# Unscaled probabilities, an output scaled behind the value product, and keys projected directly, in a fused attention and gated-FFN layer

## The reference

```
xn = layernorm(x)
q = (xn @ Wq + bq) in 8 heads of 128, + pe      # pe: sinusoidal positions
k, v = halves of (xn @ Wkv + bkv); k = k + pe   # one key/value head for all query heads
probs = softmax(causal(q @ k.T / sqrt(128)))
attn = (probs @ v) @ Wo
xr, xk = mu * xn + (1 - mu) * (xn shifted by one token)
ffn = sigmoid(xr @ Wr.T) * (relu(xk @ Wk.T) ** 2 @ Wv.T)
out = x + attn + ffn
```

## Time and profile before

| | |
|---|---|
| median of 3 runs | 1531.99 us (1531.63 to 1533.14) |
| the profiled execution | 1534.33 us |
| its span, first to last instruction | 1531.7 us |
| granted TensorE clock, mean | 0.997 |
| PE busy | 1500.0 us (98%) |
| DVE busy | 1241.5 us (81%) |
| POOL busy | 1146.9 us (75%) |
| ACT busy | 1056.0 us (69%) |

### The profile page before, as it was taken

One profiled execution on the slowest core, in us unless ns is written; L12 is line 12 of the kernel. 1 busy time (PEld: TensorE's weight loads), 2 busy tenths in 40 slices (PEclk: granted clock), 3 DMA queues, 4 the chain that ended last, 5 costly groups with the idle time before them and its releaser, 6 DMA issues.

```text
span 1531.7 us, 36132 instructions
## 1 busy us (share of the span) xinstructions
PE 1500.0 (98%) x11724; PEld 1463.2 (96%) x11724; DVE 1241.5 (81%) x3393; ACT 1056.0 (69%) x2531; POOL 1146.9 (75%) x1666
## 2 busy tenths in 40 slices
PE   6999999999999999999999999999999999999998
PEld 6999999999999999999999999999999999999998
DVE  6888868888688886888868888788877887778875
ACT  5776667766677766777577666677767766766764
POOL 5787877878677777777777777778777787767864
PEclk9999999999999999999999999999999999999999
DMA  4144422444224441234413444134441344413443
GB/s 144 39 125 125 129 94 57 129 129 138 84 61 116 138 147 63 79 114 143 130 59 94 116 140 131 45 107 118 136 140 35 101 129 134 135 33 94 125 151 104
DMA packets 227001, 165.04 MB, mean 108 GB/s; under 512 B 51712, under 2 KB 222080, under 8 KB 226816
## 3 DMA queue, kind: packets, MB, share of 16 engines
q1 hardware_dynamic: 225552, 162.08, 35.3%
q10 hardware_dynamic: 1264, 0.66, 0.2%
HBM read 81.93 MB, written 77.59 MB: 104 GB/s over the span
## 4 chain that ended last, share of the span: by engine, by line
PE 77%; DVE 7%; POOL 6%; DMA 4%; issue 3%; SPq 1%; ACT 1%; ACTq 0%; DVEq 0%; POOLq 0%
PE pS L1051 25%; PE pO L1188 21%; PE pG L1051 13%; PE pG L1138 9%; PE pT L1154 7%; DMA park_dram<-Y 3%; POOL X L581 2%; POOL qt L533 2%; SPq L461 1%; DMA Z<-park_dram 1%; DVE X L1030 1%; DVE Y L939 1%; POOL pt L548 1%; DVE mix L875 1%; DVE pt L955 1%
## 5 line engine op out<-in xcount | busy, mean ns | idle before, releaser
L1051 PE MATMUL pS<-kt,qt 128*128 128x288 f32 (+41 forms) x2304 | 460.9, 330 | 3.6 <-POOL qt L533 1.9
L782 ACT ACTIVATE X<-X,bias 128x16 f32<-128x16 f32 (+56 forms) x512 | 376.3, 735 | 112.0 <-DVE bias L1030 110.5
L1188 PE MATMUL pO<-pt,v 128*128 128x256 f32 x3288 | 441.0, 284 | 1.6 <-DVE ot L1009 1.5
L1188 PEld LDWEIGHTS pO<-pt,v 128*128 128x128 f32 x3288 | 405.8, 189 | 2.5 <-DVE ot L1009 2.3
L1030 DVE CUSTOM_DVE_ANT_0 X<-pS,mask 128x16 f32<-128x16 f32 (+56 forms) x512 | 354.0, 691 | 52.6 <-PE pS L1051 45.8
L581 POOL TENSOR_SCALAR X<-X,rec 128x16 f32<-128x16 f32 (+56 forms) x512 | 371.0, 725 | 32.7 <-DVE rec L929 22.0
L548 POOL TENSOR_TENSOR pt<-Z,pt 128x256 fp32r<-128x256 f32 (+5 forms) x192 | 318.9, 1661 | 93.4 <-ACT pt L704 89.3
L1051 PEld LDWEIGHTS pS<-kt,qt 128*128 128x128 f32 x2304 | 367.4, 189 | 16.9 <-DVE bias L1030 2.4
L775 ACT CAST ot<-pO 128x256 fp32r<-128x256 f32 x256 | 96.4, 376 | 235.7 <-PE pO L1188 119.9
L955 DVE TENSOR_TENSOR pt<-pT,pt 128x512 fp32r<-128x512 f32 (+3 forms) x440 | 207.7, 493 | 32.1 <-ACT pt L711 30.6
L533 POOL TENSOR_TENSOR qt<-qtmp,qt 128x256 fp32r<-128x256 f32 x252 | 191.3, 762 | 25.0 <-ACT qt L677 18.0
(11 more groups left out here) (120 smaller groups left out, 1931.7 us busy)
## 6 DMA issues: line engine op xcount, KB each, us to landing
park_dram<-Y SPq DMA_DIRECT2D x32, 512.0 KB, 2.6
Z<-park_dram SPq DMA_DIRECT2D x128, 128.0 KB, 2.8
park_dram<-Y SPq DMA_DIRECT2D x32, 448.0 KB, 3.0
Z<-park_dram SPq DMA_DIRECT2D x128, 112.0 KB, 2.5
park_dram<-Y SPq DMA_DIRECT2D x32, 384.0 KB, 2.9
Z<-park_dram SPq DMA_DIRECT2D x128, 96.0 KB, 2.4
park_dram<-Y SPq DMA_DIRECT2D x32, 320.0 KB, 2.7
Z<-park_dram SPq DMA_DIRECT2D x128, 80.0 KB, 2.1
```

The lines of the kernel that those rows point to most:

```text
L782: nc.scalar.activation(x_row(s, 0, w), x_row(s, 0, w), ACT.Exp, bias=bias[:, j:j + 1], scale=-1.0, accum_out=total[:, j:j + 1]).then_inc(e ...
L1051: last = nc.tensor.matmul(out, a[i], m[j], start=start and k == 0, stop=stop and k == n - 1)
L1188: last = nc.tensor.matmul(pO[:, 0:2 * P], v[i][:, k, :], pt[j][:, pair % 2, k, :], start=n == 0, stop=n == 3 * nk - 1)
```

## The change

- The probabilities are no longer scaled. POOL's scaling is gone; what is left of it in an iteration is clearing the unwritten part of a row tile, and the copies of the packed diagonal part (a copy where it was a scaling). DVE takes one reciprocal for a pair (two columns) in place of two.
- The reciprocals of a pair (128 by 2) are written to DRAM by one DMA and read back to all partitions by another (`inverse`, 128 by 256). Both stand in SP's queue, at `s+3` and `s+7` of the pair's even step.
- Behind the value product DVE multiplies `pO` by `inverse` into SBUF (`o_scaled`); ACT makes the high part from it one iteration later (`O_LAG`), POOL the low part. The next value product waits for DVE's multiplication.
- Keys are projected transposed (`wkv` stationary, tokens moving) and get bias and position there; what PE transposes is now the values, which DVE copies out. Two small key tables and their additions at the start are gone; `omu` is computed on POOL.
- The lags and tables are new (`T_LAG` 6 to 5, `V_LAG` 3 to 2), and the order in an iteration: PE does WO, transposition, fillers, scores, value product; DVE does the mask before the output's multiplication; POOL does `pt` low at its end. `Z` is a ring of four units, of which a narrow step takes one.
- ACT's copy of a PE-transposed step waits for the value product of the pair two before it.

```diff
-T_LAG = 6
+T_LAG = 5
 PV_LAG = 8
-V_LAG = 3
-H_LAG = (7, 8)
+V_LAG = 2
+H_LAG = (7, 7)
+SUMS = 2
+SUMS_AT = 3
+O_LAG = 1
...
-      "mixk_dve": (6, 11, 8, 10),
-      "mixk_out": (12, 14, 10, 11)}
+      "mixk_dve": (6, 9, 7, 10),
+      "mixk_out": (13, 13, 10, 13)}
...
+            def sums_out_of(b, s):
+                k = pair_no(b, s)
+                sp.wait_ge(rec_ready, k + 1)
+                if k >= 4:
+                    sp.wait_ge(sums_landed[(k - 4) % SUMS], 16 * ((k - 4) // SUMS + 1))
+                sp.dma_start(sums_d[k % 4, :, :], rec[:, k % 4, :]
+                             ).then_inc(sums_out[k % 2], 16)
+            def sums_in(b, s):
+                k = pair_no(b, s)
+                sp.wait_ge(sums_out[k % 2], 16 * (k // 2 + 1))
+                if k >= SUMS:
+                    sp.wait_ge(o_lo, k - SUMS + 1)
+                sp.dma_start(inverse[:, k % SUMS, :, :], sums_d[k % 4:k % 4 + 1, :, :].broadcast_to((P, P, 2))
+                             ).then_inc(sums_landed[k % SUMS], 16)
             for b, it in turns():
+                if it % 2 == SUMS_AT % 2 and 0 <= it - SUMS_AT - 4 < STEPS:
+                    sums_in(b, it - SUMS_AT - 4)
+                if it % 2 == SUMS_AT % 2 and 0 <= it - SUMS_AT < STEPS:
+                    sums_out_of(b, it - SUMS_AT)
...
-                    if not scaled_by_act(s):
-                        nc.gpsimd.tensor_scalar(x_row(s, 0, w), x_row(s, 0, w), rec[:, j:j + 1], 1.0,
-                                                ALU.mult, ALU.mult).then_inc(normed, 1)
...
+                first = it - PV_LAG - 1 - O_LAG
+                if 0 <= first < STEPS and first % 2 == 0:
+                    k = pair_no(b, first)
+                    pool.wait_ge(o_hi, k + 1)
+                    nc.gpsimd.tensor_tensor(o_out[1], scaled_o(k).rearrange("p t (h q) -> p t h q", h=H),
+                                            o_out[0].bitcast(F), ALU.subtract).then_inc(o_lo, 1)
...
                 s = it - T_LAG
                 if 0 <= s < STEPS:
+                    if t_banks(s) and pair_no(b, s) > 1:
+                        act.wait_ge(pv_done, pair_no(b, s) - 1)
...
+                first = it - PV_LAG - 1
+                if 0 <= first < STEPS and first % 2 == 0:
+                    k = pair_no(b, first)
+                    dve.wait_ge(pv_done, k + 1)
+                    dve.wait_ge(sums_landed[k % SUMS], 16 * (k // SUMS + 1))
+                    nc.vector.tensor_tensor(scaled_o(k), pO[:, 0:2 * P].rearrange("p (t n) -> p t n", t=2), scaled_o(k),
+                                            ALU.mult).then_inc(o_scaled, 1)
...
-                                pe.wait_ge(o_lo, b * (STEPS // 2) + pair)
+                                pe.wait_ge(o_scaled, b * (STEPS // 2) + pair)
```

More of the change, by code:

```diff
@@ L183, in t_banks, with z_units @@
     return [] if turned(s) else [(k, min(4, n - k)) for k in range(0, n, 4)]
+def z_units():
+    unit, before, used = [], [], [None] * UNITS
+    for n in range(2 * len(TURNED)):
+        s = TURNED[n % len(TURNED)]
+        size = 1 if s < SHARED else 2
+        ends = n and unit[n - 1] + (1 if TURNED[(n - 1) % len(TURNED)] < SHARED else 2)
+        u = 0 if n % len(TURNED) == 0 else -(-ends // size) * size % UNITS
+        users = [x for x in used[u:u + size] if x is not None]
+        unit.append(u)
+        before.append(n - max(users) if users else 0)
+        used[u:u + size] = [n] * size
+    return unit[0:len(TURNED)], before
 def users_before():
@@ L209 @@
 T_BODY = T_FIRST[STEPS]
-N_FIRST = [sum((SUB * 2 if packed(r) else P) > (r % H + 1) * SUB for r in range(s))
-           + sum((not scaled_by_act(r)) + packed(r) for r in range(s)) for s in range(STEPS + 1)]
+N_FIRST = [sum(((SUB * 2 if packed(r) else P) > (r % H + 1) * SUB) + packed(r) for r in range(s))
+           for s in range(STEPS + 1)]
 N_BODY = N_FIRST[STEPS]
@@ new lines, in turn @@
+                if 0 <= s < STEPS and s % 2:
+                    k = pair_no(b, s)
+                    dve.wait_ge(exp_done, b * STEPS + s + 1)
+                    if k >= 4:
+                        dve.wait_ge(sums_out[k % 2], 16 * ((k - 4) // 2 + 1))
+                    nc.vector.reciprocal(rec[:, k % 4, :], total[:, k % 4, :]).then_inc(rec_ready, 1)
+                s = it - T_LAG
+                for w in [w for w in WITHIN if w + H_LAG[w % 2] + 1 == it]:
+                    last = w // H
+                    dve.wait_ge(turned_hi, turned_no(b, w) + 1)
+                    within = pt_of(0, w)[32:64, last, :].rearrange("p (a c) -> p a c", a=4)
+                    nc.vector.tensor_tensor(within, z_of(w, last + 1)[32:64, :, last, :], within.bitcast(F),
+                                            ALU.subtract).then_inc(within_lo, 1)
@@ new lines, in turn @@
+                if 0 <= s < STEPS:
+                    for m, (k, nk) in enumerate(t_banks(s)):
+                        u = T_FIRST[s] + m
+                        dve.wait_ge(t_hi, b * T_BODY + u + 1)
+                        full = nk - (packed(s) and k + nk == s // H + 1)
+                        if full:
+                            low = nc.vector.tensor_tensor(pt_of(1, s)[:, k:k + full, :],
+                                                          pT[u % 2][:, 0:full * P].rearrange("p (k n) -> p k n", n=P),
+                                                          pt_of(0, s)[:, k:k + full, :].bitcast(F), ALU.subtract)
+                        if full < nk:
+                            within = pt_of(0, s)[32:64, s // H, :]
+                            low = nc.vector.tensor_tensor(within, pT[u % 2][32:64, full * P:nk * P], within.bitcast(F),
+                                                          ALU.subtract)
+                        low.then_inc(t_lo, 1)
```

436 lines of the change are left out of this document (199 added, 237 removed).

## The result

| | before | changed |
|---|---|---|
| median | 1531.81 us (1530.04 to 1533.14) | 1776.12 us (1765.07 to 1780.68, 4 runs) |
| ratio, 95% interval | | 1.159 (1.157 to 1.161), slower |
| span of the profiled execution | 1531.7 us | 1763.3 us |
| PE idle in it | 31.7 us | 176.8 us |
| granted clock, mean | 0.997 | 0.967 |

A forecast was written before the change was run, and what follows sets the result against it. PE was taken as the bound, at work 1500.0 of 1531.7 us. Terms -8.7 - 1.5 - 2.4 - 2.0 + 0.45 + 1.2 = -13.0 took the profiled 1534.3 to 1521.3, the median to 1519.0 us; range 1509 to 1538.

The forecast's parts named there:

- The two DMAs of a pair: SP's queue: 512 added DMAs, the read issued some 6 us before DVE needs it; hidden, 0.
- Rival C: Spread sums come late, so DVE sits before `pO` and PE's value product behind it: 17 us, 1536; chance 0.08.
- The sign of B: In PE's list, waits of scores for DVE's `bias` or mask of more than 5 us.
- POOL: POOL's busy time falls from 1146.9 to about 971 us; FK's wait for its mix split goes, -8.7 us.
- rival A: The stall changes its owner: DVE or ACT late where POOL was, about 1530 us; chance 0.17.
- The order: PE's WO first in its iteration, fewer waits for its bank: -2.4 us; all terms together -13.0.
- rival B: Narrow steps wait for their mask behind value product, ACT's copy and DVE: 25.6 us lost, 1544.6; chance 0.11.
- dense time fixed: PE's 1500.0 us of work stay, with products as many and as wide; at most 31.7 us idle can go.
- DVE: Fewer reciprocals, a new copy of transposed values: net -27 us, busy 1205 to 1225 us, 0 on the path.
- The start: `omu` and key table leave DVE's path; POOL's mix split at 20.48 and FK come earlier: -2.0 us.
- The end: WO of the last row tile comes later, as DVE's multiplication goes first: +0.45 us.
- The clock: With PE's 1.9 us pause before the FK at 1402, the slow stretch behind it goes: -1.5 us.

The follow-up runs named there:

- e2: Changed kernel with only the write of the reciprocals, read back left out, output multiplied by a constant tile: 1744.8 us.
- e1: Changed kernel without its two small DMAs per pair, output multiplied by a constant tile instead of the reciprocals: 1553.5 us.
- e3: Changed kernel with only the read back, of a constant 1 KB row broadcast to all partitions, nothing written: 1553.7 us.
- f10: Changed kernel with the write alone, in packets of 64 bytes side by side, constant factor: 1553.8 us.
- f11: Changed kernel with the write alone, 8-byte packets each 512 bytes from the next in DRAM, constant factor: 1553.1 us.
- f9: Kernel before with POOL's split of the token mix of chunk 2 one iteration earlier: 1539.8 us.
- e7: Changed kernel without its small DMAs, constant factor, PE's value product put back ahead of the scores: 1578.8 us.
- f12: Changed kernel without its small DMAs, constant factor, WO put back behind transposition and other fillers: 1585.5 us.
- e8: Kernel before with an added write per pair, 128 packets of 8 bytes side by side to DRAM, read by nobody: 1802.1 us.
- e4: Changed kernel with both small DMAs issued from ScalarE's (ACT's) queue instead of SP's: 1853.5 us.

## Why the prediction was wrong

**The step that failed** is "The two DMAs of a pair": "None so small and so often is in the trace; the nearest land in 1.9 us (32 KB), a large one in 3.0 us ... hidden, 0." The step asked only when the new DMAs land and who waits for them. It never asked what they do to the transfers already there. The runs put this in its place: the write costs 191 us (`e2` less `e1`), with a parking that lands at 5.8 in place of 3.6 us, and the read, which costs 0.2 us alone, another 31 us beside it (changed kernel less `e2`); there it lands in 4.7 us, and DVE's multiplication waits 298.6 us for it. That it queues behind the slow writes is likely and was not tried. The 32 KB row was the wrong neighbour: the read moves 128 KB and alone lands in 3.5 us (`e3`); in `f10` and `f11` small writes do land in 1.9 us, as it says, and only 8-byte ones side by side don't. The text had a bound for lost cover, "up to 1.9 us" a pair, which over 256 pairs is 486 us; it was not carried into the range. Rival C named the place, SP's ordered list and `pO` waiting for `inverse`, at 17 us and 0.08, but not the slow writes as its cause. The sign of B (scores waiting for DVE's `bias`, 18.6 us) is not in PE's list of `e1`, so it followed from the DMAs.

**What let a slow transfer through to the end** is the ring in SP's queue, and the prediction read SP only for the new waits. The kernel before already waited at the fetch for its parking, on SP's own list of waits:

```profile
SPq L461 <- DMA park_dram<-Y: 263.6, 145, 3.8
```

Its ring of 4.8 us against 5.98 had about 1.1 us of slack (an estimate, as above), and 2.5 us more landing were added.

**POOL: right in size, wrong in worth.** Its busy time is 968.0 us (971 forecast), the low part of the output 768 ns on average (762 from the earlier trace rows). FK no longer waits for POOL behind the start. But the -8.7 us were not won: `f9` makes just this move and loses 7 us with a wait for DVE in its place. The mechanism of rival A, for which the text had 0.17, shows there; its time, about 1530, did not come.

**The order lost 22 us where it was to gain 13.** `e1` holds this apart from the DMAs. PE's list there names small waits only, the largest of them these:

```profile
PE pG L1176 <- ACT ot L818: 7.4, 9, 1.1
PE pT L1195 <- DVE pt L1032: 6.1, 15, 1.0
```

The first is WO of iteration 34, for ACT's copy of the output: the dependence that DVE's multiplication ahead of the copy made a hand-over longer. The second is DVE's part of a PE-transposed narrow step, near to rival B's place, not the mask that B had. The prediction allowed 1.0 us for that WO, behind XT in the bank; it waits for ACT, 0.79 us in each element, 6.3 us in all. PE's idle time of `e1` is 32.5 us (1552.1 - 1519.6) against 31.7 before, so nearly all of the 20 us stand inside PE's busy time, which has grown from 1500.0 to 1519.6 with the same 11724 products. Gaps too short to be drawn would do that, and so would products that take a little longer (the score products have a mean of 335 ns, 330 before); the profile does not tell them apart. The step that held PE's "dense time fixed" failed by these 20 us. Which edit brings them stays open; `e7` and `f12` only exclude two.

**DVE: wrong.** 1256.0 us, 1263.7 in `e1`, where 1205 to 1225 were forecast. The reciprocals went (80.2 to 40.2 us in `e1`), but other instructions became longer. The normalized tokens, before and in `e1`:

```profile
L826 DVE SCALAR_TENSOR_TENSOR xn<-xtok,mv,rstd 128x256 f32<-128x256 f32 x64 | 37.6, 628 | 0.5
```
```profile
L862 DVE SCALAR_TENSOR_TENSOR xn<-xtok,mv,rstd 128x256 f32<-128x256 f32 x64 | 57.8, 943 | 0.6 <-POOL rstd L562 0.6
```

With the product by the gate (`xtok<-gate,xtok`, 30.5 us before and 45.0 in `e1`) this adds 34.7 us; why they became longer was not tried. The mix of the earlier trace rows did not: its median is 480 ns in all three kernels, its mean 686 before, 612 in `e1` and 713 in the changed kernel. The key split, now from SBUF, has a median of 488 ns and a maximum of 1330 in `e1`, against 424 and 425 from PSUM. Its direction is the one that the Trainium skill's rule gives ("SBUF — State Buffer", "SBUF: two separate sides"), but of the 24 us that the 32 splits could have waited 8 came (21.4 us in `e1`, 13.4 before). Of the two stretched rows that the prediction reads by this rule, only the mixes have two SBUF inputs; `omu` has one, so its 2.40 us are not a case of the rule as it is told there.

**The start: right.** From the timeline of the changed kernel, for 20.48 us in the earlier trace rows:

```profile
18.51 1.27 POOL L588 TENSOR_TENSOR mh<-mix,mh 128x512 fp32r<-128x512 f32 x1
```

2.0 us earlier, as said. In `e1` it is at 19.20, 1.3 us earlier.

**The end: right.** From DVE's multiplication on, in the changed kernel:

```profile
1757.02 0.41 ACT L822 CAST ot<-inverse 128x256 fp32r<-128x256 f32 x1 [3.22 <-DVE inverse L1073]
...
1757.58 3.04 PE L1180 MATMUL pG<-wo,ot 128*128 128x256 f32 x24 [1.05 <-ACT ot L822]
```

PE waited 1.05 us for its last WO where it waited 0.55: +0.5 for +0.45.

**The clock: right in `e1`, not in the changed kernel.** In `e1` the only stretch at the lower level is at the start, so what the earlier trace rows has at 1402 to 1406 is gone, as forecast. But this stretch at the start is longer, in one execution: 0.50 from 26 to 34 us and 0.73 and 0.71 on both sides, where the kernel before has 0.83 and then 0.50 from 28 to 34. A pause taken from one place does not say what the clock gives elsewhere. In the changed kernel the mean fell to 0.967, with PE idle for 177 us. By the clock's records 116 us of its span stand at 0.50, against 10 before, which is up to 53 us more of PE's busy time (an estimate: half of the 106). Its busy time grew by 86.5 us, 1500.0 to 1586.5, and 20 of them are those of `e1`. `e1`, without the waits, has a mean of 0.997; so this part of the loss came with the waits, though no run held the clock apart.

## What to carry to other kernels

Before adding a DMA, ask what it does to the DMAs that run beside it, and find the ring of issue, landing and fetch that has the least slack; a transfer's cost can be another's delay. A reduction of one small value per partition should not go to DRAM as neighbouring 8-byte packets: set them apart by 512 bytes (tried for the write alone), or gather them into one SBUF row first (1555 against 1776 us here). And when a wait names an engine, try the one-number edit that takes the wait away before counting it as gain; here it came back as a wait for the next engine.

## What the runs showed of the hardware

- A write of 128 packets of 8 bytes, side by side in 1 KB of DRAM, made 512 KB writes beside it land in 5.8 us in place of 3.6 (`e2`, `e1`), or 5.9 in place of 2.6 in the kernel before (`e8`), with the 128 KB fetches from DRAM nearly unchanged at 3.0 and 2.8 us. Not every read was spared: in `e8` a 256 KB load landed in 5.8 in place of 3.3 us. Issued from ACT's queue it did not spare the parking (`e4`: 6.8 us). Its own landing grew to between 3.5 and 5.4 us.
- 64-byte packets side by side (`f10`) and 8-byte packets 512 bytes apart (`f11`) land in 1.9 us and leave the 512 KB parking at 3.6 and 3.7 us. Why 8-byte packets side by side are slow is not shown: the runs fit the theory in the expectation of `f11`, packets of different DMA engines in the same small block, but none looked at the memory itself, and packets of 16 or 32 bytes were not tried.
- PE's busy share can hide a loss: 98% in the kernel before and in `e1`, with 20 us between their spans.
